# Values times output weights of the second layer, two batches in one product

## The chip, the cores and the metric

The kernel runs on one core of one Trainium2 chip. Its time is the device time of one execution in microseconds (us), taken as the median of 3 runs. The profiled execution is one more execution, of which every row in this document is read. Engines are named as in the profile: PE is TensorE (matmuls), PEld its weight loads, DVE is VectorE, ACT is ScalarE, POOL is GpSimd, SP issues most DMAs.

## What is computed

Four transformer layers on x (4 batches, 256 tokens, 256 features), each a cross-attention on a context of 64 rows per batch and a feed-forward block. The change is in the second layer's attention (L1), of which this is the part that matters:

```python
kv_c = kv @ W_kvc                                  # compressed context, 64 features
k_nope = (kv_c @ W_uk).reshape(b, lk, H, HD)       # H = 16 heads of HD = 128
v = (kv_c @ W_uv).reshape(b, lk, H, HD)
k_rope = rope(kv_c @ W_kr)                         # one for all heads
scores = (q_nope . k_nope + q_rope . k_rope) * scale
attn = softmax(where(good, scores, NEG))
out = einsum('bhqk,bkhd->bqhd', attn, v).reshape(b, lq, H * HD)
return out @ W_o
```

The kernel multiplies each head's values by that head's rows of W_o ahead of the softmax: vo[head, batch] = (kv_c W_uv[head]) W_o[head], 64 context rows by 256 outputs. These tables depend on the context alone and are made long before the second layer begins. They are kept in `a1_vo`, two heads of a pair in one tile of 128 rows: rows 0 to 63 the even head, rows 64 to 127 the odd one.

## The kernel before

The program is written out by hand: every engine has its own instruction order, and semaphores tie them together. A wait holds up all that is behind it on its engine. Helpers such as `products` (line 200) and `turns` (line 209) record most matmuls and transposes, so those have one line for many places.

Three places make the tables of the second layer's attention:

1. Early values, in layer 0's attention (about 34 to 59 us). `layer1_compress_scalar` copies kv_c to `kvc` (line 431). Then heads 0 to 7 pass through a pipeline: PE makes the values of one head (line 487, one product of 256 context columns), ACT copies them to `a_vhead` (line 516), PE multiplies by the output weights (line 498), and ACT copies to `a_vo` (line 506). Line 498 makes one product for each batch: the 64 context rows of the batch are the stationary operand, 256 columns of weights stream. Two batches share a bank, and ACT copies two batches at once: so four products and two copies a head. A product of 32-bit floats leaves two records in the profile, so line 498 has 64 records for 32 products.
2. Keys, in layer 0's feed-forward block (about 65 to 77 us): products of folded weights (line 449) and of `kvc` (line 458), and eight copies on ACT to `a_kq` (line 473).
3. Late values, heads 8 to 15, a step at a time in the loop over the 32 experts of layer 0 (about 125 to 191 us). A head is three steps of the loop: values (line 539), the products of batches 0 and 1, and those of 2 and 3 (line 546). The eight heads take 24 rounds of the loop.

What stands behind the early values: on ACT, in its order, the normalised rows of layer 0's feed-forward (line 304); on PE the transposes of all rows (line 209), then the gate (16 tiles, 32 records, line 200), whose copy on DVE (line 726) begins the routing. DVE and POOL make the other rows (lines 287 and 324). The expert loop gathers rows on POOL (line 1127), and adds the results on POOL (line 1135) by indirect DMAs. In the second layer, DVE sets `a_key_blocks` (line 1341), the block-diagonal rotated keys.

## Time and profile before

| | |
|---|---|
| median of 3 runs | 1147.77 us (1147.11 to 1149.47) |
| profiled execution, span from first to last instruction | 1144.6 us |
| PE busy | 1017.9 us, 89% of the span |
| ACT busy | 632.5 us, 55% |
| DVE busy | 758.7 us, 66% |

The profile gives the profiled execution by its span; its device time is not listed beside it. The median of the runs is 3.2 us above the span, which is taken as what lies around it. A timeline row has start, length, engine, line, operation, and in brackets the idle time of the engine before it and what ended it. The busy share of PE says how full it is over the whole program; what a change of one stage is worth has to be read from the waits of that stage.

### The profile page before, as it was taken

The page shows a single profiled execution, that of the slowest core. Times are in us where ns is not written, and L with a number is a line of the kernel's source. Part 1 is how long each engine was busy: PE and PEld are TensorE (multiplying, and loading weights), DVE is VectorE, ACT ScalarE, POOL GpSimd, SP SyncE. Part 2 cuts the span into 40 slices and gives each one's busy share as a digit, 9 for nine tenths or more (in the row PEclk, how much of TensorE's full clock was granted, in tenths as well). Part 3 has the DMA queues.
Part 4 walks back from the last instruction along what each step waited for, and adds up shares of the span by engine and source line. Part 5 has one row for each costly group of instructions (what it writes and reads, how often), then busy time and mean ns, then how long its engine had stood idle before and what let it go on. Part 6 is the DMA issues. An engine that isn't in the chain of part 4 may idle for free. (4 is left out here: it accounts for less than half of the span.)

```text
span 1144.6 us, 18785 instructions
## 1 busy us (share of the span) xinstructions
PE 1017.9 (89%) x6173; PEld 821.7 (72%) x6173; DVE 758.7 (66%) x2019; ACT 632.5 (55%) x1824; POOL 525.5 (46%) x582
## 2 busy tenths in 40 slices
PE   4987998198998878899999999999999999998997
PEld 2473555156687657788888888989899777677785
DVE  3757222276657347878888888787877689677444
ACT  1341443002124436779787878888888745553253
POOL 1341677254555353334545454444443236452453
PEclk9999999599998898889999999999999999998999
DMA  9130798920004863010102010102000034005674
GB/s 389 50 125 14 190 220 216 251 60 1 1 1 162 273 220 130 1 60 1 61 1 61 1 61 2 60 2 61 1 24 2 1 125 131 1 1 193 216 277 158
DMA packets 57264, 108.89 MB, mean 95 GB/s; under 512 B 13840, under 2 KB 35216, under 8 KB 55248
## 3 DMA queue, kind: packets, MB, share of 16 engines
q1 hardware_dynamic: 47920, 89.71, 23.8%
q0 software_dynamic: 9248, 18.00, 6.1%
q8 instruction: 49, 0.80, 0.3%
q14 instruction: 47, 0.39, 0.1%
HBM read 79.19 MB, written 27.42 MB: 93 GB/s over the span
## 5 line engine op out<-in xcount | busy, mean ns | idle before, releaser
L3028 POOL TENSOR_TENSOR a_p<-a_p,a_tot 128x128 f32<-128x128 f32 x64 | 50.9, 814 | 204.2 <-DVE a_tot L2650 204.2
L200 PE MATMUL bank<-a_w_high,a_in 128*128 128x128 f32 (+1 forms) x512 | 124.4, 285 | 9.6 <-DVE a_in L2167 4.7
L200 PE MATMUL bank<-a_w_low,a_in 128*128 128x128 f32 (+1 forms) x512 | 120.8, 282 | 0.0
L200 PEld LDWEIGHTS bank<-a_w_high,a_in 128*128 128x128 f32 x512 | 99.0, 193 | 12.3 <-DVE a_in L2167 4.5
L200 PEld LDWEIGHTS bank<-a_w_low,a_in 128*128 128x128 f32 x512 | 99.3, 194 | 0.0
L209 PE MATMUL bank<-const 128*128 128x128 f32 x433 | 63.9, 311 | 32.6 <-DVE x L1045 20.5
L209 PEld LDWEIGHTS bank<-const 128*128 128x128 f32 x433 | 59.0, 164 | 36.9 <-DVE x L1045 21.3
L2701 DVE TENSOR_REDUCE a_top<-bank 128x2 f32<-128x512 f32 (+1 forms) x96 | 56.8, 600 | 29.7 <-PE bank L2489 18.0
L2863 ACT ACTIVATE a_qn<-bank,a_q_shift,a_q_rstd 128x128 f32<-128x128 f32 x128 | 48.3, 461 | 40.0 <-POOL a_q_shift L262 40.0
L2679 DVE TENSOR_SCALAR a_qn<-bank,a_qk_minus,a_qk_rstd 128x128 f32<-128x128 f32 x192 | 64.0, 402 | 5.5 <-POOL a_qk_rstd L259 2.8
L200 PE MATMUL bank<-a_proj_high,a_catq 128*128 128x256 f32 x256 | 63.9, 288 | 1.0 <-issue 1.0
L2936 ACT ACTIVATE a_cat<-bank,l_ismooth 128x256 bf16<-128x256 f32 x128 | 50.3, 481 | 23.3 <-PE bank L2529 23.3
L2489 PE MATMUL bank<-a_kt,a_qt 128*128 128x256 f32 x256 | 62.3, 386 | 0.0
L1940 DVE SCALAR_TENSOR_TENSOR f_swi_inner<-bank,f_swi_gated 128x128 f32<-128x128 f32 x78 | 22.4, 290 | 59.5 <-ACT f_swi_gated L1052 59.5
L200 PE MATMUL bank<-a_proj_low,a_catq 128*128 128x256 f32 x256 | 61.7, 279 | 0.0
L200 PE MATMUL bank<-cols,a_vs 128*128 128x256 f32 x256 | 61.1, 382 | 0.0
L2914 ACT ACTIVATE a_p<-bank,a_top 128x256 f32<-128x256 f32 x128 | 59.0, 477 | 0.0
L259 POOL TENSOR_TENSOR rstd<-var,const 128x4 f32<-128x4 f32 x18 | 19.4, 1079 | 85.3 <-DVE minus_mean L253 85.3
L1052 ACT ACTIVATE f_swi_gated<-bank 128x128 f32<-128x128 f32 x78 | 21.5, 277 | 64.8 <-PE bank L200 64.6
L1168 ACT ACTIVATE soft_pt<-bank 128x512 f32<-128x512 f32 x32 | 17.4, 595 | 69.4 <-PE bank L209 69.4
L2855 ACT ACTIVATE a_p<-a_p,a_tot 128x256 f32<-128x256 f32 x128 | 55.5, 540 | 0.0
L209 PE MATMUL bank<-const,a_p 128*128 128x128 f32 x320 | 46.8, 283 | 8.1 <-DVE a_qn L2679 7.4
(427 smaller groups left out, 3039.5 us busy)
## 6 DMA issues: line engine op xcount, KB each, us to landing
experts<-in_experts SPq DMA_DIRECT2D x49, 384.0 KB, 4.4
f_expert<-in_experts SPq DMA_DIRECT2D x31, 384.0 KB, 5.5
third_shelf<-in_groups SPq DMA_DIRECT2D x8, 1024.0 KB, 6.5
f_got<-f_xs SPq DMA_DIRECT2D x10, 516.0 KB, 8.1
third_shelf<-in_groups SPq DMA_DIRECT2D x8, 512.0 KB, 4.3
f_got<-f_ys SPq DMA_DIRECT2D x8, 512.0 KB, 5.3
f_xs<-blank_zero SPq DMA_DIRECT2D x1, 3999.0 KB, 21.3
l_expert<-in_experts SPq DMA_DIRECT2D x10, 384.0 KB, 6.9
```

The lines of the kernel that those rows point to most:

```text
L200: ins = pe.matmul(out, lhs, rhs, start=start and n == 0, stop=stop and n == len(pairs) - 1, skip_group_check=shared)
L209: ins = k.pe.transpose(o, i, ident[0:i.shape[0], 0:i.shape[0]])
L1052: k.a.activation(m.gated[n % 3][0:rows, :], k.bank[n % 3][0:rows, 0:I], ACT.Silu, scale=1.0).then_inc(*s["swi_gated"].one())
L1940: v.scalar_tensor_tensor(m.inner[n % 3][:], bank[n % 3][:, I:2 * I], share, m.gated[n % 3][:], ALU.mult, ALU.mult).then_inc(*s["swi_inner" ...
L2489: ins = pe.matmul(bank[5 + ti][:, h * S:(h + 1) * S], q[:, h, ti * P:(ti + 1) * P], kt[:], start=True, stop=True)
L2679: ins = v.tensor_scalar(dst[i], src[i], m.stats_qk.minus[:, i:i + 1], m.stats_qk.rstd[:, i:i + 1], ALU.add, ALU.mult)
L2701: v.tensor_reduce(top[:, cs], src, AX.X, ALU.max, negate=True).then_inc(*s["top_ready"].one())
L2855: ins = a.activation(p[:, h, :], p[:, h, :], ACT.Copy, scale=tot[:, c:c + 1])
L2863: ins = a.activation(m.qn[:, 0, c, :], bank[3][:, c * P:(c + 1) * P], ACT.Identity, bias=m.stats_q.shift[:, c:c + 1], scale=m.stats_q.rstd ...
L2914: ins = a.activation(own_probs(m, ti)[:, h, :], bank[5 + ti][:, h * S:(h + 1) * S], ACT.Exp, bias=top[:, c:c + 1], accum_out=tot[:, c:c + 1])
L2936: ins = a.activation(m.cat[n % 2][:, c * S:(c + 1) * S], bank[h][:, part * S:(part + 1) * S], ACT.Copy, scale=m.ismooth[:, ch:ch + 1])
L3028: g_.tensor_tensor(cross_probs(m, ti), cross_probs(m, ti), over(m.tot[n % 2][:, first:first + HPG], SC), ALU.mult).then_inc(*s["cross_weig ...
```

## The change

For each head one product now takes the 128 context rows of two batches as the stationary operand. Its output has the first batch of the two in rows 0 to 63 of a bank and the second in rows 64 to 127. To keep the two heads of a pair in the two halves of one tile, the odd heads are made from a copy of kv_c in which the two batches of each couple are exchanged (`kvc_crossed`, two more copies on ACT). So in batches 0 and 2 the even head lies in the upper half of a pair's tile, in batches 1 and 3 the odd head does. The keys follow: within a pair the two heads are exchanged in batches 1 and 3, for `a_kq` by the place to which the key products write and two half-size copies for one, for `a_key_blocks` by four instructions in place of two. Copies to `a_vo` stay two for each head, each of 64 rows by 512. A late head is now two steps of the expert loop, and ACT makes both its copies in one step.

```diff
--- before.py
+++ after.py
@@ -428,6 +428,9 @@
 def layer1_compress_scalar(k, s):
     k.on_a.wait_ge(*s["kvc_made"].at(1))
+    sides = lambda ap: ap.rearrange("p (c d s) -> p c d s", c=B // 2, d=2)
+    for d in range(2):
+        k.a.activation(sides(k.kvc_crossed[:])[:, :, d, :], sides(k.bank[5][0:KVC, 0:CTX])[:, :, 1 - d, :], ACT.Copy)
     k.a.activation(k.kvc[:], k.bank[5][0:KVC, 0:CTX], ACT.Copy).then_inc(*k.kvc_copied.one())
@@ -453,10 +456,12 @@
         bank = k.bank[KEY_BANKS[n % len(KEY_BANKS)]]
         on.wait_ge(*s["fold_copied"].at(max(2 * n // FOLD, n % len(KEY_BANKS)) + 1))
         on.wait_ge(*k.kq_scaled.at(n - len(KEY_BANKS) + 1))
+        kvc = k.kvc[:].rearrange("p (c d s) -> p d c s", c=B // 2, d=2)
+        parts = bank[0:QC, :].rearrange("p (q c s) -> p q c s", q=4, c=B // 2)
         for i in range(2):
             h = 2 * n + i
-            ins = pe.matmul(bank[0:QC, i * CTX:(i + 1) * CTX], fold[:, h * QC:(h + 1) * QC], k.kvc[:], start=True,
-                            stop=True)
+            ins = pe.matmul(parts[:, 1:3, :, :] if i else parts[:, 0:4:3, :, :], fold[:, h * QC:(h + 1) * QC], kvc,
+                            start=True, stop=True, skip_group_check=True)
         ins.then_inc(*s["keys_made"].one())
@@ -470,8 +475,10 @@
 def layer1_keys_scalar(k, s):
     for n in range(H1 // 2):
         k.on_a.wait_ge(*s["keys_made"].at(n + 1))
-        k.a.activation(k.kq[:, :, 2 * n:2 * n + 2, :], k.bank[KEY_BANKS[n % len(KEY_BANKS)]][0:QC, :].rearrange(
-            "p (h b s) -> p b h s", h=2, b=B), ACT.Copy, scale=SOFT1).then_inc(*k.kq_scaled.one())
+        bank = k.bank[KEY_BANKS[n % len(KEY_BANKS)]][0:QC, :].rearrange("p (d h c s) -> p d c h s", d=2, h=2, c=B // 2)
+        for d in range(2):
+            ins = k.a.activation(k.kq[:, d::2, 2 * n:2 * n + 2, :], bank[:, d, :, :, :], ACT.Copy, scale=SOFT1)
+        ins.then_inc(*k.kq_scaled.one())
 def layer1_values_tensor(k, s, pair_free):
@@ -484,27 +491,33 @@
     for r in range(EARLY + 1):
         if r < EARLY:
             on.wait_ge(*s["vhead_copied"].at(r - 1))
-            pe.matmul(k.bank[6 + r % 2][:, 0:CTX], uv[:, r, :], k.kvc[:], start=True,
+            pe.matmul(k.bank[6 + r % 2][:, 0:CTX], uv[:, r, :], kept_context(k, r), start=True,
                       stop=True).then_inc(*s["vhead_made"].one())
         if r >= 1:
             i = r - 1
-            lo = (i % 2) * SC
             on.wait_ge(*s["vhead_copied"].at(i + 1))
-            for pair in range(B // 2):
-                n = 2 * i + pair
-                on.wait_ge(*(pair_free[n] if n < 4 else k.vo_copied.at(n - 3)))
-                for b in range(2):
-                    at = (pair * 2 + b) * SC
-                    ins = pe.matmul(k.bank[1 + n % 4][lo:lo + SC, b * D:(b + 1) * D], k.vhead[i % 3][:, at:at + SC],
-                                    wo[:, i, :], start=True, stop=True)
-                ins.then_inc(*s["wo_made"].one())
-def value_out_scalar(k, h, pair, bank):
-    lo = (h % 2) * SC
-    k.a.activation(k.vo[lo:lo + SC, pair * 2:pair * 2 + 2, h // 2, :],
-                   bank[lo:lo + SC, :].rearrange("p (b d) -> p b d", b=2), ACT.Copy).then_inc(*k.vo_copied.one())
+            on.wait_ge(*(pair_free[i] if i < 4 else k.vo_copied.at(2 * (i - 3))))
+            value_out_tensor(k, s, i, wo[:, i, :], k.bank[1 + i % 4])
+def kept_context(k, h):
+    return k.kvc_crossed[:] if h % 2 else k.kvc[:]
+def value_out_tensor(k, s, i, wo, bank):
+    for c in range(B // 2):
+        ins = k.pe.matmul(bank[:, c * D:(c + 1) * D], k.vhead[i % 3][:, c * P:(c + 1) * P], wo, start=True, stop=True)
+    ins.then_inc(*s["wo_made"].one())
+def value_out_scalar(k, h, bank):
+    for side in range(2):
+        part, d = slice(side * SC, (side + 1) * SC), (side + h) % 2
+        k.a.activation(k.vo[part, d::2, h // 2, :], bank[part, :].rearrange("p (c d) -> p c d", c=B // 2),
+                       ACT.Copy).then_inc(*k.vo_copied.one())
 def layer1_values_scalar(k, s):
@@ -512,51 +525,44 @@
     for r in range(EARLY + 1):
         if r < EARLY:
             on.wait_ge(*s["vhead_made"].at(r + 1))
-            on.wait_ge(*s["wo_made"].at(2 * (r - 2)))
+            on.wait_ge(*s["wo_made"].at(r - 2))
             a.activation(k.vhead[r % 3][:], k.bank[6 + r % 2][:, 0:CTX],
                          ACT.Copy).then_inc(*s["vhead_copied"].one())
         if r >= 1:
-            for pair in range(B // 2):
-                n = 2 * (r - 1) + pair
-                on.wait_ge(*s["wo_made"].at(n + 1))
-                value_out_scalar(k, r - 1, pair, k.bank[1 + n % 4])
-LATE = 3 * (H1 - EARLY)
+            on.wait_ge(*s["wo_made"].at(r))
+            value_out_scalar(k, r - 1, k.bank[1 + (r - 1) % 4])
+LATE = 2 * (H1 - EARLY)
 def late_value_tensor(k, s, step, bank):
     pe, on = k.pe, k.on_pe
-    i, part = divmod(step, 3)
-    lo = ((EARLY + i) % 2) * SC
+    i, part = divmod(step, 2)
     if part == 0:
         on.wait_ge(*k.l1_in)
         on.wait_ge(*k.vo_copied.at(2 * (EARLY + i)))
         uv = k.l1["uv_late"][0:KVC, :].rearrange("p (h d) -> p h d", d=HD1)
-        pe.matmul(bank[:, 0:CTX], uv[:, i, :], k.kvc[:], start=True, stop=True).then_inc(*s["vhead_made"].one())
+        pe.matmul(bank[:, 0:CTX], uv[:, i, :], kept_context(k, EARLY + i), start=True,
+                  stop=True).then_inc(*s["vhead_made"].one())
     else:
         wo = k.l1["wo_late"].rearrange("p (h d) -> p h d", d=D)
         on.wait_ge(*s["vhead_copied"].at(i + 1))
-        on.wait_ge(*k.vo_copied.at(2 * (EARLY + i) + part - 1))
-        for b in range(2):
-            at = ((part - 1) * 2 + b) * SC
-            ins = pe.matmul(bank[lo:lo + SC, b * D:(b + 1) * D], k.vhead[i % 3][:, at:at + SC], wo[:, i, :],
-                            start=True, stop=True)
-        ins.then_inc(*s["wo_made"].one())
+        value_out_tensor(k, s, i, wo[:, i, :], bank)
 def late_value_scalar(k, s, step, bank):
-    i, part = divmod(step, 3)
+    i, part = divmod(step, 2)
     if part == 0:
         k.on_a.wait_ge(*s["vhead_made"].at(i + 1))
-        k.on_a.wait_ge(*s["wo_made"].at(2 * (i - 2)))
+        k.on_a.wait_ge(*s["wo_made"].at(i - 2))
         k.a.activation(k.vhead[i % 3][:], bank[:, 0:CTX], ACT.Copy).then_inc(*s["vhead_copied"].one())
     else:
-        k.on_a.wait_ge(*s["wo_made"].at(2 * i + part))
-        value_out_scalar(k, EARLY + i, part - 1, bank)
+        k.on_a.wait_ge(*s["wo_made"].at(i + 1))
+        value_out_scalar(k, EARLY + i, bank)
 VALUES = dict(pe="vhead_made wo_made", a="vhead_copied")
@@ -1338,8 +1344,10 @@
     on.wait_ge(*step.now())
     on.wait_ge(*s["keys_zeroed"].at(1))
     for h in range(2):
-        ins = v.tensor_scalar(m.key_blocks[h * R1:(h + 1) * R1, :, h * SC:(h + 1) * SC],
-                              by_b(m.turn_a[h * R1:(h + 1) * R1, :]), SOFT1, None, ALU.mult)
+        for d in range(2):
+            at = (h + d) % 2
+            ins = v.tensor_scalar(m.key_blocks[h * R1:(h + 1) * R1, d::2, at * SC:(at + 1) * SC],
+                                  by_b(m.turn_a[h * R1:(h + 1) * R1, :])[:, d::2, :], SOFT1, None, ALU.mult)
     ins.then_inc(*s["keys_set"].one())
     def rotate(half):
@@ -3586,6 +3594,7 @@
         k.expert_in, k.experts_first = [k.landing(f"expert{n}_in") for n in range(SLOTS)], 0
         k.route1 = sparse_routing(k, SPARSE1, ctx)
         k.kvc = k.sb("a1_kvc", [KVC, CTX], scope=l1_scope)
+        k.kvc_crossed = k.sb("a1_kvc_crossed", [KVC, CTX], scope=l1_scope)
         k.kq = k.sb("a1_kq", [QC, B, H1, SC], scope=l1_scope)
         k.vo = k.sb("a1_vo", [P, B, H1 // 2, D], scope=l1_scope)
         l1 = k.sb("l1_weights", [P, width(L1A)], scope=l1_scope)
```

How the order changes on PE in the early values, from the compression (line 200) on. Before, line 487 makes values and line 498 multiplies by output weights:

```order
L200 MATMUL bank<-ctxt,l_key_weights 64x256 x2
L487 MATMUL bank<-a_kvc,l_value_weights 128x256 x2
L498 MATMUL bank<-l_value_weights,a_vhead 64x256 x4
L487 MATMUL bank<-a_kvc,l_value_weights 128x256
L498 MATMUL bank<-l_value_weights,a_vhead 64x256 x4
L487 MATMUL bank<-a_kvc,l_value_weights 128x256
L498 MATMUL bank<-l_value_weights,a_vhead 64x256 x4
```

The same place of the changed kernel (lines 494 and 511 do this now):

```order
L200 MATMUL bank<-ctxt,l_key_weights 64x256 x2
L494 MATMUL bank<-a_kvc,l_value_weights 128x256
L494 MATMUL bank<-a_kvc_crossed,l_value_weights 128x256
L511 MATMUL bank<-l_value_weights,a_vhead 128x256 x2
L494 MATMUL bank<-a_kvc,l_value_weights 128x256
L511 MATMUL bank<-l_value_weights,a_vhead 128x256 x2
L494 MATMUL bank<-a_kvc_crossed,l_value_weights 128x256
```

The order of the heads is the same; each group of four products with 64 output rows is a group of two with 128 output rows.

How the order changes on ACT, from the last instruction ahead of the compressed context on. Before:

```order
L660 ACTIVATE l_seq<-bank,l_weights 128x256 x2
L431 ACTIVATE a_kvc<-bank 64x256
L516 ACTIVATE a_vhead<-bank 128x256 x2
L506 ACTIVATE a_vo<-bank 64x2x256 x2
L516 ACTIVATE a_vhead<-bank 128x256
```

The same place of the changed kernel:

```order
L433 ACTIVATE a_kvc_crossed<-bank 64x2x64 x2
L434 ACTIVATE a_kvc<-bank 64x256
L529 ACTIVATE a_vhead<-bank 128x256 x2
L519 ACTIVATE a_vo<-bank 64x2x256 x2
L529 ACTIVATE a_vhead<-bank 128x256
```

Two copies stand ahead of that of kv_c, and the rest keeps its order.

How the order changes on PE in the expert loop, at the first late head (line 539 makes its values, line 546 multiplies). Before:

```order
L539 MATMUL bank<-a_kvc,l_weights 128x256
L209 MATMUL bank<-const,f_pick 128x96 x2
L200 MATMUL bank<-experts,f_cols 96x256 x2
L209 MATMUL bank<-const,swi_inner 128x96
L931 MATMUL bank<-experts,swi_turned 96x256
L546 MATMUL bank<-l_weights,a_vhead_2 64x256 x2
L209 MATMUL bank<-const,f_pick 128x96 x2
L200 MATMUL bank<-experts,f_cols 96x256 x2
L209 MATMUL bank<-const,swi_inner 128x96
L931 MATMUL bank<-experts,swi_turned 96x256
L546 MATMUL bank<-l_weights,a_vhead_2 64x256 x2
```

The same place of the changed kernel:

```order
L549 MATMUL bank<-a_kvc,l_weights 128x256
L209 MATMUL bank<-const,f_pick 128x96 x2
L200 MATMUL bank<-experts,f_cols 96x256 x2
L209 MATMUL bank<-const,swi_inner 128x96
L937 MATMUL bank<-experts,swi_turned 96x256
L511 MATMUL bank<-l_weights,a_vhead_2 128x256 x2
L209 MATMUL bank<-const,f_pick 128x96 x2
L200 MATMUL bank<-experts,f_cols 96x256 x2
L209 MATMUL bank<-const,swi_inner 128x96
L937 MATMUL bank<-experts,swi_turned 96x256
L549 MATMUL bank<-a_kvc_crossed,l_weights 128x256
```

One round of every three no longer has late work of its own: 16 rounds have it, not 24.

## Rows read from the trace of the kernel before

**Rows 1.** Timeline, PE, ahead of the early values (start, length, engine, line, what)

```profile
19.38 2.07 PE L200 MATMUL bank<-l_weights,l_mean_wide 128*128 128x256 f32 x4 [3.68 <-DVE l_mean_wide L627]
21.38 1.22 PE L200 MATMUL bank<-l_weights,const 1*128 1x256 f32 x2
22.53 2.08 PE L200 MATMUL bank<-l_weights,l_mean_wide 128*128 128x256 f32 x4
```

**Rows 2.** Timeline of PE and ACT in the early values, heads 0 to 2

```profile
33.99 0.38 ACT L431 ACTIVATE a_kvc<-bank 64x256 f32<-64x256 f32 x1 [17.42 <-PE bank L200]
...
36.49 3.67 PE L498 MATMUL bank<-l_value_weights,a_vhead 128*64 128x256 f32 x8
...
38.49 0.59 ACT L506 ACTIVATE a_vo<-bank 64x512 f32<-64x512 f32 x1 [1.51 <-PE bank L498]
...
41.24 3.67 PE L498 MATMUL bank<-l_value_weights,a_vhead 128*64 128x256 f32 x8
...
45.54 1.94 PE L498 MATMUL bank<-l_value_weights,a_vhead 128*64 128x256 f32 x8
```

**Rows 3.** Timeline, a later head, the end of the early values, and ACT's rows

```profile
48.04 1.94 PE L498 MATMUL bank<-l_value_weights,a_vhead 128*64 128x256 f32 x8
...
49.15 0.59 ACT L506 ACTIVATE a_vo<-bank 64x512 f32<-64x512 f32 x1 [0.62 <-PE bank L498]
...
50.53 1.49 PEld L498 LDWEIGHTS bank<-l_value_weights,a_vhead 128*64 128x64 f32 x8 [0.33 <-issue]
...
54.60 1.32 POOL L324 TENSOR_SCALAR rows<-x,minus_mean,rstd 128x256 f32<-128x256 f32 x2
...
57.51 1.69 ACT L506 ACTIVATE a_vo<-bank 64x512 f32<-64x512 f32 x3 [0.27 <-PE bank L498]
59.22 1.09 ACT L304 ACTIVATE rows<-x,shift,rstd 128x256 f32<-128x256 f32 x2
```

**Rows 4.** Timeline, transposes, gate, and the key copies

```profile
60.03 1.94 PE L209 MATMUL bank<-const,rows 128*128 128x128 f32 x16 [1.64 <-issue]
...
61.88 3.73 PE L200 MATMUL bank<-l_weights,cols 128*128 128x32 f32 x32
...
65.71 0.42 DVE L726 COPY f_logits<-bank 128x256 f32<-128x256 f32 x1 [3.45 <-PE bank L200]
...
75.39 0.59 ACT L473 ACTIVATE a_kq<-bank 96x512 f32<-96x512 f32 x1 [0.27 <-PE bank L458]
```

**Rows 5.** Stretches of PE: start:end, length, busy (records), granted clock, DMA share, GB/s

```profile
19.38:22.53 3.15, 3.15 (x7) 1.00 1.03 402
...
41.24:44.90 3.66, 3.66 (x10) 1.00 0.00 0
...
61.85:65.50 3.65, 3.65 (x34) 1.00 1.06 346
65.50:68.90 3.40, 3.40 (x22) 0.50 0.98 359
227.85:232.70 4.85, 4.82 (x23) 0.50 1.10 322
```

**Rows 6.** Timeline, fill transposes at either pace, and PE's wait for the mask

```profile
77.01 7.21 PE L209 MATMUL bank<-const 128*128 128x128 f32 x64
...
87.61 0.28 PE L869 MATMUL bank<-f_mask,f_before 128*128 128x256 bf16 x1 [3.39 <-DVE f_mask L982]
...
227.88 5.62 PE L209 MATMUL bank<-const 128*128 128x128 f32 x28 [20.53 <-DVE x L1045]
```

**Rows 7.** Expert loop: timeline of POOL and a small ACT copy; a line of the waits

```profile
124.07 0.27 ACT L1052 ACTIVATE swi_gated<-bank 96x128 f32<-96x128 f32 x1 [2.15 <-PE bank L200]
...
175.95 1.44 POOL L1135 DMA_INDIRECT sum<-f_ys,f_index  x1 [0.30 <-ACT f_ys L1100]
...
178.93 1.44 POOL L1135 DMA_INDIRECT sum<-f_ys,f_index  x1 [0.30 <-DMA sum<-f_ys,f_index]
...
ACT f_ys L1100 <- DMA sum<-f_ys,f_index: 23.7, 12, 3.6
```

## Prediction

> **What bounds the kernel here.** I read the timeline of the three places that the change touches, then PE's pace in stretches, then the waits of the expert loop. In the early values PE is the bound: ACT's copies to `a_vo` wait for PE (1.51 us, later 0.62 us), and ACT ends them at 57.51 + 1.69 = 59.20 [rows 2, 3]. Only then can ACT make its rows (59.22), which the transposes at 60.03 wait for, though POOL had its last rows ready at 54.60 + 1.32 = 55.92 [rows 3, 4]. Transposes, gate and routing follow in one chain to DVE's copy at 65.71. So a us at the end of the early values is a us of the kernel, down to a floor: with ACT early, POOL's rows (the first of the two ends near 55.3) let the transposes begin at about 55.5, 4.5 us sooner.
>
> The reader must see a second thing, PE's pace. A group of eight records of 256 columns takes 3.67 us at 36.49 and 41.24, and 1.94 us from 45.54 on [rows 2]. That is the lower and the higher level of PE's clock, 1.2 and 2.4 GHz; the granted clock is printed as 1.00 even in the slow stretches (19.38 and 41.24), so here the durations tell the level [rows 5]. What had PE done? From 19.38 on it worked in groups of four records and two, with a pause at each border: 22.53 - 19.38 = 3.15 us for six records, which at 0.427 each ((3.67 - 1.94)/8 = 0.216 is what a record loses, so 0.43 is the low pace) are 2.56 us of work [rows 1, 2]. It printed as busy throughout and stayed slow for 25 us. It rose right after the second unbroken group of eight. Later, at 65.5, the clock fell behind the gate, whose products have only 32 columns, and was up again at 77, after denser work [rows 4 to 6].
>
> **The change, part by part.**
>
> Two copies of `kvc` with exchanged batches stand ahead of the one that starts the values. The trace has none of 64 x 128; an ACT copy of 96 x 128 takes 0.27 [rows 7], 64 x 256 takes 0.38 [rows 2]. Two cost 0.4 to 0.76; I take 0.5. PE's first output product moves from 36.49 to 37.0.
>
> The output products. Four records of 128 stationary columns stand where eight of 64 did; a record is paid by its 256 streamed columns, as the wide stationary of rows 1 and the narrow one of rows 2 both run at 0.43 at the low pace. At the high pace a head took 50.53 - 48.04 = 2.49 us [rows 3] and would take 2.49 - 4 x 0.216 = 1.63. At the low pace a head took 41.24 - 36.49 = 4.75 [rows 2] and would take what the six records of rows 1 take, 3.15.
>
> The question is which pace PE gets, and this decides the sign. With the change no group of eight is left before the last head: each round is four records, a pause, two records, a pause, and the two are of 64 rows only. This is the pattern of rows 1, which never brought the clock up, not that of 41.24, after which it rose. So I take the low pace for all the early values.
> - Output products of head 0 at 37.0, of head 6 at 37.0 + 6 x 3.15 = 55.9, of head 7 right behind at 55.9 + 4 x 0.43 = 57.6. A first copy starts 2.0 behind its group's start (38.49 - 36.49) [rows 2]: 59.6. Two copies take 1.1 (three took 1.69) [rows 3]. End 60.7 instead of 59.2: +1.5.
> - Transposes: 61.88 - 60.03 = 1.85 for 16 before [rows 4]. A low transpose is 5.62/28 = 0.20, a high one 7.21/64 = 0.11 [rows 6]: 16 x 0.20 = 3.2. +1.4.
> - Gate: 3.73 for 32 records, 0.117 each [rows 4]. That is the pace of a 128-column transpose, so the load of 128 stationary columns rather than the 32 streamed ones seems to set it, and it would become 0.20: 6.4. +2.7. No row shows a gate at the low clock. If something else sets the 0.117, the term is 0.
> - Sum 1.5 + 1.4 + 2.7 = +5.6, with the clock low to the end of the gate. But the last two heads' output products are now together an unbroken eight records (55.9 to 59.3), and the 16 transposes are an unbroken 3.2. Either can bring the clock up as the eight at 41.24 did; then part of the 4.1 of transposes and gate goes. I take off 1.6: +4.0.
>
> The Trainium skill has a rule against the change: in "TensorE: Matmul & The Clock Gate", section "A second HAM failure mode: psum-queue depth-cycling", short idles of PE between groups of matmuls are said to cost it the higher clock. By that rule the early values run slow; the rows above agree as far as groups of four and two go. The same page, section "Step-by-step: what each phase is for", gives 62 ns of sequencer time for a MATMUL; an estimate by it makes the gate bound by issue, with no growth at the low clock, and the sum +2.9 or less.
>
> The keys. ACT's eight copies of 96 x 512 (0.59, each behind a wait of 0.27 for PE) become sixteen of 96 x 256, a pair about 2 x 0.38 = 0.76, inside the 0.86 that PE takes for a pair [rows 4]. Only the last pair ends later, by 0.2; PE then waits 3.39 for the mask, which covers it [rows 6]. The writes of the key products in pieces of 64 columns: 0, or, if it slowed them by a tenth, 0.7, under the same cover. If PE were still slow in the keys, 7 us would be added to 3.4 of slack; but the folded weights ahead of them are dense, and brought the clock up before [rows 5].
>
> `a_key_blocks`: two instructions more on DVE, 0.1 each; PE rotates queries meanwhile and DVE catches up. 0, or +0.2.
>
> The late values. Eight heads lose two products each, 16 x 0.43 = 6.9 us of PE. POOL sets the loop's pace: its additions come 178.93 - 175.95 = 2.98 apart, and ACT's copies of results wait 23.7 us in 12 times for those DMAs [rows 7]. So PE's saving is hidden: 0. ACT makes both copies in one step, 0.5 more in that round and less in others, under the same cover. If PE were the bound, -6.9; if ACT's longer step delayed additions, +1.
>
> **The sum** against the profiled execution is 1144.6 + 4.0 = 1148.6 of span. With the 3.2 us around it that stand between its span and the median, 1147.77 + 4.0 = 1151.8.
>
> **The rivals.**
>
> *The clock rises as before* (PE keeps working nearly all the time, and it rose at 45). Then heads 0, 1 and 2 start at 37.0, 40.2 and 43.3, head 3 at 46.1, and from there 1.63 a head: head 6 at 51.0, head 7 at 51.9, first copy 1.11 later (49.15 - 48.04) [rows 3], end 54.1. Now POOL's rows bind, transposes at 55.5 instead of 60.0: -4.5, 1143.3. Against it: the pattern of rows 1. For it: PE is printed as busy through all of it, and one rise is little to judge by. Chance 0.22.
>
> *The gain comes in the expert loop*, PE's 6.9 us counting in full on top of +4.0: 1144.9. Against it POOL's 2.98 [rows 7]. Chance 0.03.
>
> *The clock rises in the last eight records and stays up* through transposes and gate: only the 1.5 is left, 1149.3, within the noise. The pause behind them (ACT's two copies and its row, about 2 us) speaks against it. Chance 0.12.
>
> **How the numbers follow.** The forecast, low clock through the early values and in part or all of what follows, has 0.63; its own range is 1150.2 to 1154.0 (+2.4, the clock up from the transposes' end, to +6.2, with the dearer copies and all terms). The range for 8 in 10 reaches from 1144.0, into the early-rise case, to 1154.0. About 0.2% (2.3 us) can be told from no change here. Faster 0.25, same 0.13, slower 0.62.
>
> **What would show it.** In the profile after: groups of four output records (line 511) with about 2.0 us each, heads 3.1 apart to the end; ACT's last copy of the early values near 60.7; transposes of 0.2 and a gate of over 5 us; DVE's copy of the logits near 69 to 71 instead of 65.7. The additions on POOL should still be 2.98 apart, with PE's idle share in the loop larger. The prediction is wrong if line 511 runs in groups of 1.1 us from about 45 on and the transposes start near 55.5; and its mechanism is wrong if the logits come no later than before and the loss lies in the expert loop or behind.

## The result, and the profile after

| kernel | runs | median us | range us |
|---|---|---|---|
| before | 6 | 1148.24 | 1147.11 to 1149.47 |
| after | 6 | 1155.65 | 1151.13 to 1158.98 |

The ratio is 1.0065, 95% interval [1.0047, 1.0083]: slower by 7.4 us, where 4.0 were forecast and 1154.0 was the end of the range. The profiled execution of the changed kernel was its fastest (1151.13 us, span 1149.6); the kernel before had a span of 1144.6. A second profile of each was taken later with unchanged code (spans 1153.9 and 1148.1), and the table below has all four. It gives the us from one event to the next, in order of time (starts, but for the first row); the columns add up to the spans to within 0.1.

| from the event before to | before | before, again | after | after, again |
|---|---|---|---|---|
| end of ACT's last early copy to `a_vo` | 59.2 | 59.1 | 60.5 | 60.8 |
| DVE's copy of the logits | 6.5 | 6.5 | 7.1 | 11.3 |
| first product with the mask | 21.9 | 21.9 | 21.9 | 21.9 |
| POOL's first gather | 22.9 | 22.9 | 23.9 | 24.0 |
| POOL's first addition | 17.7 | 17.7 | 21.1 | 21.0 |
| POOL's last addition | 81.9 | 82.8 | 81.7 | 81.4 |
| end | 934.5 | 937.2 | 933.5 | 933.6 |

All of the loss is ahead of the first addition: 6.2 us in the first pair (134.42 instead of 128.2), 10.9 in the second. Behind it 1.2 and 5.1 us came back, so that the spans are 5.0 and 5.8 us apart; no run explains that part. The early values answer as forecast. The timeline of the changed kernel (start, length, engine, line, what):

```profile
33.72 0.43 ACT L433 ACTIVATE a_kvc_crossed<-bank 64x128 f32<-64x128 f32 x2 [17.43 <-PE bank L200]
...
36.53 2.07 PE L511 MATMUL bank<-l_value_weights,a_vhead 128*128 128x256 f32 x4
38.64 1.21 ACT L519 ACTIVATE a_vo<-bank 64x512 f32<-64x512 f32 x2 [1.62 <-PE bank L511]
...
39.69 2.08 PE L511 MATMUL bank<-l_value_weights,a_vhead 128*128 128x256 f32 x4
...
52.30 2.07 PE L511 MATMUL bank<-l_value_weights,a_vhead 128*128 128x256 f32 x4
...
55.45 3.78 PE L511 MATMUL bank<-l_value_weights,a_vhead 128*128 128x256 f32 x8
...
59.27 1.21 ACT L519 ACTIVATE a_vo<-bank 64x512 f32<-64x512 f32 x2 [0.50 <-PE bank L511]
60.50 1.09 ACT L304 ACTIVATE rows<-x,shift,rstd 128x256 f32<-128x256 f32 x2
```

Beside [rows 2, 3]: no group ever takes 1.1 us; heads start 3.15 apart from 36.53 to 52.30, on half the records and all at the lower level, where the kernel before had 1.94 for eight records from 45.54 on. The two crossed copies took 0.43 us. Transposes, gate and logits, here and (second fence) in the second execution:

```profile
61.31 1.94 PE L209 MATMUL bank<-const,rows 128*128 128x128 f32 x16 [2.08 <-issue]
...
63.15 4.31 PE L200 MATMUL bank<-l_weights,cols 128*128 128x32 f32 x32
...
67.57 0.42 DVE L732 COPY f_logits<-bank 128x256 f32<-128x256 f32 x1 [4.03 <-PE bank L200]
...
73.94 0.65 ACT L480 ACTIVATE a_kq<-bank 96x256 f32<-96x256 f32 x2 [0.55 <-PE bank L463]
```

```profile
61.60 3.65 PE L209 MATMUL bank<-const,rows 128*128 128x128 f32 x16 [2.08 <-issue]
65.04 6.87 PE L200 MATMUL bank<-l_weights,cols 128*128 128x32 f32 x32
...
72.02 0.42 DVE L732 COPY f_logits<-bank 128x256 f32<-128x256 f32 x1 [6.90 <-PE bank L200]
```

Beside [rows 4]: the clock rose at 59.3 in the first execution, just behind the last eight output records, and not before 77 in the second. In the second, the gate takes 6.87 us for 3.73: the dearer of the two prices that the prediction gave it. Stretches of the changed kernel (start:end, length, busy, then the granted clock, the DMA share, GB/s):

```profile
36.52:52.30 15.78, 15.78 (x32) 8.37 (x31) 14.94 (x44) 7.67 (x15) 7.12 (x10) 0.50 0.14 48
59.28:66.10 6.82, 4.79 (x43) 4.71 (x43) 1.38 (x2) 3.46 (x6) 5.12 (x12) 1.00 0.45 149
66.10:72.90 6.80, 6.80 (x40) 6.51 (x40) 0.87 (x3) 4.82 (x8) 6.80 (x3) 0.50 1.00 351
113.90:117.30 3.40, 3.40 (x10) 2.61 (x10) 0.59 (x3) 0.77 (x3) 2.52 (x3) 0.50 0.26 68
127.60:131.00 3.40, 3.40 (x10) 2.35 (x11) 0.66 (x3) 0.27 (x1) 0.00 (x0) 0.50 0.91 361
```

The last two are what the prediction did not look at. They lie between the first gather and the first addition, where PE has the shared expert's products and then those of the first gathered rows. The clock fell there for 3.4 us twice. The first product of gathered rows in the kernel before:

```profile
122.96 1.07 PE L200 MATMUL bank<-experts,f_cols 128*96 128x256 f32 x4 [0.38 <-DVE f_cols L1031]
```

and after:

```profile
127.53 1.97 PE L200 MATMUL bank<-experts,f_cols 128*96 128x256 f32 x4 [0.38 <-DVE f_cols L1037]
```

In the expert loop, POOL's additions keep their pace. From the first to the last of them PE is busy for 62.2 us of 81.7, where it was 71.2 of 81.9: PE's saving of the late values became waiting.

```profile
176.24 1.44 POOL L1141 DMA_INDIRECT sum<-f_ys,f_index  x1 [0.31 <-DVE swi_inner L1044]
...
179.22 1.44 POOL L1141 DMA_INDIRECT sum<-f_ys,f_index  x1 [0.30 <-issue]
```

ACT's waits for those additions, over the whole program (us, times, longest), were 30.2 in 15 times before; the 23.7 of [rows 7] are those up to 200 us only:

```profile
ACT f_ys L1106 <- DMA sum<-f_ys,f_index: 38.5, 16, 4.3
```

### The profile page after: what moved, and what is told of

Its sections match the earlier page's. It is cut to its first block and busy times, and to the rows that moved or that the text cites. A ratio compares the mean times of both kernels' runs of the same rounds, so it can differ in the third digit from the quotient of the medians.

```text
span 1149.6 us, 18669 instructions
## 1 busy us (share of the span) xinstructions
PE 1013.0 (88%) x6109; PEld 824.8 (72%) x6109; DVE 758.5 (66%) x2021; ACT 632.8 (55%) x1834; POOL 525.5 (46%) x582
## 3 DMA queue, kind: packets, MB, share of 16 engines
q1 hardware_dynamic: 47920, 89.71, 23.9%
## 5 line engine op out<-in xcount | busy, mean ns | idle before, releaser
L209 PE MATMUL bank<-const 128*128 128x128 f32 x433 | 60.8, 300 | 33.8 <-DVE x L1051 21.5
L209 PEld LDWEIGHTS bank<-const 128*128 128x128 f32 x433 | 55.3, 157 | 37.8 <-DVE x L1051 21.9
L200 PE MATMUL bank<-cols,a_vs 128*128 128x256 f32 x256 | 60.5, 380 | 0.0
L259 POOL TENSOR_TENSOR rstd<-var,const 128x4 f32<-128x4 f32 x18 | 19.4, 1079 | 85.1 <-DVE minus_mean L253 85.1
L2863 ACT ACTIVATE a_p<-a_p,a_tot 128x256 f32<-128x256 f32 x128 | 55.5, 539 | 0.0
```

Source lines behind the costliest of these rows:

```text
L200: ins = pe.matmul(out, lhs, rhs, start=start and n == 0, stop=stop and n == len(pairs) - 1, skip_group_check=shared)
L209: ins = k.pe.transpose(o, i, ident[0:i.shape[0], 0:i.shape[0]])
L2863: ins = a.activation(p[:, h, :], p[:, h, :], ACT.Copy, scale=tot[:, c:c + 1])
```

## The experiments

Ratios are to the kernel before, run in the same session (its medians there were 1146.2 to 1147.4; one execution of it, of 3477 us, is in no ratio), with 95% intervals. "The change" is the changed kernel. "..." marks lines of an edit that are left out here. Where two kernels of one pair are compared, the difference of their means is worked out from their runs, with twice its error.

**One. Undo the products' form.** In the changed kernel each product of 128 rows becomes two of 64, in the early values (first), the late ones (second), or both (third).

```
...
-        ins = k.pe.matmul(bank[:, c * D:(c + 1) * D], k.vhead[i % 3][:, c * P:(c + 1) * P], wo, start=True, stop=True)
+        for d in range(2 if split else 1):
+            n = SC if split else P
+            at = c * P + d * n
+            ins = k.pe.matmul(bank[d * n:(d + 1) * n, c * D:(c + 1) * D], k.vhead[i % 3][:, at:at + n], wo,
+                              start=True, stop=True)
...
```

> The changed kernel, with each early output product (heads 0 to 7) made again as two products of 64 rows, each to its half of the same bank; all else as changed. Pace theory: groups of eight records are back, PE rises to its higher level within the early values as before, ACT's last copy ends near 59 to 60, the logits are copied near 66, and the time is 1147 to 1150. Rival, the late values (both copies in one step of the expert loop) cost the time: 1154 to 1157, as the changed kernel. Rival, the side changes (exchanged copies of kv_c, key copies halved) cost it: also 1154 to 1157.

> The changed kernel, with each late output product (heads 8 to 15, in the expert loop) made as two products of 64 rows; early ones as changed. Pace theory: 1154 to 1157, as the changed kernel, with groups of four at 2.08 us to the end of the early values. Rival, a PE that is too idle in the expert loop loses its pace there and costs the time: 1148 to 1151.

> The changed kernel with all output products split in two of 64 rows: PE's work as before, all side changes and the late order as changed. Pace theory: 1147 to 1150, as the early split alone. Rival, side changes or the order of ACT's late copies: 1154 to 1157.

Measured: 1151.06 us, 1.0037 [1.0022, 1.0051]; 1153.37, 1.0048 [1.0029, 1.0067]; 1149.89, 1.0030 [1.0013, 1.0046]. The second is just below its range of 1154 to 1157. The third lies in the range of the pace theory (1147 to 1150) and the first just above it, but not for the theory's reason, for neither is an undoing at all. The early values' timeline of the first:

```profile
36.74 1.97 PE L514 MATMUL bank<-l_value_weights,a_vhead 128*64 128x256 f32 x8
38.64 1.22 PE L494 MATMUL bank<-a_kvc,l_value_weights 64*128 64x256 f32 x2
39.79 1.97 PE L514 MATMUL bank<-l_value_weights,a_vhead 128*64 128x256 f32 x8
```

Eight records take 1.97 us at the lower level, where eight of the kernel before took 3.67 [rows 2]: the two products of a pair write to different halves of the bank's rows and run at the same time, while before, both batches of a head went to the same half. So PE is as short of work as with the change, and its clock stayed low through the early values: to 73.5 in the first, to 59.2 in the third, whose transposes and most of whose gate then ran at the higher level. Why both are 3 to 4 us nearer to the kernel before than the change (1.0065, and 1.0073 in its second session) is not shown: ACT's last early copy ends only 0.5 us sooner (60.0 and 59.9). For the late values the form makes no difference that the intervals can tell.

**Two. Give PE back its work.** Each early output product of the changed kernel is made twice in a row.

```
...
-    for c in range(B // 2):
+    for c in [c for c in range(B // 2) for _ in range(times)]:
...
```

> Each early output product is made twice in a row into the same place, so that TensorE has again eight records of 256 columns without a break per head, as before, while everything else is the change's (the second product repeats the first; nothing else differs). Theory (a dense group of eight brings the clock up): groups of 3.67 us for the first heads, the clock up by about 45, groups of 1.94 from there, ACT's last copy to a_vo at 59 to 60, logits at 65 to 67, time 0.998 to 1.002 of before: more work and yet faster than the change. Rival 1 (TensorE's clock is not decided by the pattern of work here): it stays low, eight heads of 4.75 us end at 76, and the time is 15 us above before. Rival 2 (the loss of the change is the two copies to kvc_crossed or ACT's form of the output copies): the clock rises and the time is still 1.005 of before.

Measured: 1150.13 us, 1.0036 [1.0017, 1.0055]; by its means 4.3 +- 2.0 us faster than the change in the same session, though it makes the early output products twice, and 3.3 +- 2.1 slower than the kernel before. Its PE:

```profile
36.40 3.77 PE L511 MATMUL bank<-l_value_weights,a_vhead 128*128 128x256 f32 x8
40.10 0.70 PE L494 MATMUL bank<-a_kvc,l_value_weights 64*128 64x256 f32 x2
40.73 1.99 PE L511 MATMUL bank<-l_value_weights,a_vhead 128*128 128x256 f32 x8
...
59.28 2.48 PE L209 MATMUL bank<-const,rows 128*128 128x128 f32 x16 [2.08 <-issue]
61.56 6.87 PE L200 MATMUL bank<-l_weights,cols 128*128 128x32 f32 x32
```

The clock rose at 40.0, at the end of the first group. The forecast of the time (0.998 to 1.002) missed: the clock fell again at 60.5, in the transposes, and the gate took 6.87, so the logits came at 68.5. PE's idle time ahead of the transposes is 2.08 here and with the change, 1.64 before [rows 4]; whether that made it fall is argued, since in one execution of the change, and in the third kernel of experiment one, it stayed up behind the same wait.

**Three. The order alone, in the kernel before.** The next head's value product is cut into two of 128 columns, one ahead of each pair of batches, so that eight output records become four and four.

```
...
+            at = slice(part * P, (part + 1) * P)
+            ins = pe.matmul(k.bank[6 + r % 2][:, at], uv[:, r, :], k.kvc[:, at], start=True, stop=True)
...
             for pair in range(B // 2):
+                if pair == 1:
+                    head(r, 1)
...
```

> The kernel before, without any fill, and only its order changed: the next head's value product is made in two halves of 128 columns, one ahead of each pair of batches, so that the eight output records of a head are two groups of four with a short product of 64 rows between them. The sum of the work is the same but for the switches. Theory (TensorE's clock rises on an unbroken group of eight records and not on groups of four): it stays low through the early values, a head takes 5.1 us, eight end at about 77, 15 to 18 us later than before: 1.012 to 1.016 of before. Rival (what counts is how much of the time is spent in products of 128 rows, broken or not; the change lowered that share by halving them): the clock rises between 40 and 50 as before, and the time is 1.001 to 1.004 of before.

Measured: 1150.36 us, 1.0037 [1.0021, 1.0054]. Its PE:

```profile
38.58 1.97 PE L507 MATMUL bank<-l_value_weights,a_vhead 128*64 128x256 f32 x4
40.48 0.79 PE L488 MATMUL bank<-a_kvc,l_value_weights 64*128 64x128 f32 x2
41.20 1.74 PE L507 MATMUL bank<-l_value_weights,a_vhead 128*64 128x256 f32 x4
42.87 0.48 PE L488 MATMUL bank<-a_kvc,l_value_weights 64*128 64x128 f32 x2
43.28 1.08 PE L507 MATMUL bank<-l_value_weights,a_vhead 128*64 128x256 f32 x4
```

The clock rose at 42.6 without any unbroken eight of output records. My theory of the unbroken group falls, and the rival's number (1.001 to 1.004) holds. What PE did ahead of each rise within the early values is the same in the four executions that have one (the kernel before twice, this one, and that of experiment two): the output products of a head take the time of eight records one after the other (3.94 us of a head's 5.25 here). In the five without a rise (the change twice, the three of experiment one) they take the time of four (2.07 of 3.15 with the change, 1.97 of 3.05 in the first of experiment one). These nine executions show it; that it is the cause rests on them alone. The rule that the prediction cited from the Trainium skill, "TensorE: Matmul & The Clock Gate", section "A second HAM failure mode: psum-queue depth-cycling", blames short idles between groups. This kernel has twice as many borders between groups of output products as the one before and its clock rose earlier (42.6, not 45.0), so by this case the number of pauses doesn't decide.

**Four. Bring the clock up by other means, with and without the change.** 18 transposes into a free bank go behind the product of the sequence summaries, where PE waits for DVE.

```
     ins.then_inc(*s["seq_made"].one())
+    pass_time(k, k.bank[7], 18)
```

> The changed kernel, with 18 fill transposes on PE between the first products and the summaries, where PE waits 3.7 us for DVE (about 15.7 to 19.4 us). Pace theory: PE gets to its higher level near 18 and holds it through groups of four and two; summaries take 7 us instead of 12.6, heads 1.6 us instead of 3.15, DVE and POOL then set the start of the transposes at about 49 to 51 us, and the time is 1139 to 1145. Rival, the level does not hold in groups of four and two: it falls back by 25 us, and the time is 1153 to 1157. Rival, the loss is in the expert loop: the logits come 10 us earlier but the time only by that less 3 to 5 us of loss in the loop.

> The kernel before with 18 idle-time transposes behind the product of the sequence summaries, the same that brought the changed kernel's clock up from 17.3 us on and its time to 0.9965 of before. With the clock up in both, this pair tells what the change is worth in itself. Early values at the high pace from head 0: 2.49 us a head before against 1.69 with the change, so ACT's last copy to a_vo at about 33.7 + 8 x 2.5 + 2 = 49 instead of 42.9; POOL's rows (ready near 50 then) hide that. Theory (the saving of the output products is hidden behind POOL's rows once the clock is up): 0.9955 to 0.998 of before, no more than 1.5 us from the changed kernel with the same fill. Rival (the change has a cost of its own, in the keys or the late values): 2 us or more faster than that kernel, 0.9945 or less.

Measured, with the change: 1143.73, 0.9965 [0.9945, 0.9985]. Without it: 1140.12, 0.9943 [0.9923, 0.9963]. The clock is up from about 17 us on in both, so the early values end at 42.9 and 47.4, and both wait for POOL's rows at 49.7. The groups of four and two that never raised the clock keep it up here, from 29.2 to the end of the early values. Only in the filled kernels can the saving of the output products be seen: 4.5 us, all of it waiting. With the change, PE idles 8.16 us, its clock falls at 44.6, and the transposes and the gate are at the lower level throughout (logits at 60.2). Without it PE idles 3.06 us, the clock falls at 50.8, in the transposes, and the gate is as slow (logits at 59.0). The means are 3.4 +- 2.2 us apart, which is the number of the rival (the change has a cost of its own) and not the theory's 1.5. In the profiles 1.1 us of it are there at the logits, and 3.6 more came between gather and addition (21.3 and 17.7 us), where the clock of the kernel with the change was low in two stretches and that of the other in none. The transposes with the change:

```profile
48.70 1.32 POOL L324 TENSOR_SCALAR rows<-x,minus_mean,rstd 128x256 f32<-128x256 f32 x2
49.73 3.65 PE L209 MATMUL bank<-const,rows 128*128 128x128 f32 x16 [8.16 <-POOL rows L324]
```

**Five. Cover that idle time too** (60 transposes with the change, 24 without), and then (third and fourth) also the waits ahead of the mask, of the shared experts' weights and of their first inner product.

```
+    pass_time(k, k.bank[7], 60)
     turn_rows_tensor(k, s, k.rows, rows_of(s), k.x_ready[NT - 1])
...
-    pass_time(k, k.bank[4], 64)
+    pass_time(k, k.bank[4], 82)
...
+    pass_time(k, k.bank[0], 16)
     slot, came = expert_slot(k, 0)
...
+            pass_time(k, k.bank[7], 14 if r == 1 else 0)
             on.wait_ge(*s["swi_inner"].at(i + 1))
```

> The change, with 18 idle-time transposes behind the sequence summaries (as in the two earlier pairs) and 60 more in TensorE's idle time of 8 us ahead of the row transposes, where the clock fell. Theory (transposes and gate take 1.85 + 3.73 at the higher clock): row transposes at 49.7, logits at about 55.4 instead of 60.2, so 4.8 us less than with the first fill alone: 0.9915 to 0.994 of before. Where the shared experts fall into a stretch of low clock, 3 us of it go again. Rival (the fill delays the row transposes or the clock falls all the same): logits at 60 or later, 0.9965 or more.

> The kernel before with the same two fills, the second of 24 transposes, since TensorE is idle only 3.06 us there. Theory: logits at about 55.4 instead of 59.0, 3.6 us less than with the first fill alone, 0.990 to 0.993 of before, and within 1.5 us of the changed kernel with two fills (TensorE's shorter early values end in waiting for POOL's rows). Rival (the change has a cost of its own beside the clock): 2 us or more faster than the changed kernel with two fills.

> The change with those two fills and three more places covered: 82 transposes instead of 64 ahead of the mask, 16 between the last picks and the shared experts' weights, 14 in the wait for the first inner product. Theory (the 3 us that the shared experts took longer in some executions are TensorE's clock, which falls in these waits): mask to first gather 22.9, first gather to first addition 17.7 instead of 21, 0.988 to 0.991 of before, the fastest of the changed ones. Rival (that stretch is longer by the change itself, for instance by DMAs): 21 us again with the clock up throughout.

> The kernel before with all five fills. Theory (with the clock held up everywhere ahead of the expert loop the change is worth nothing either way, since POOL's rows and POOL's additions bound both): within 1.5 us of the changed kernel with all fills, first addition at the same time within 1 us. Rival 1 (the change costs by itself): 2 us or more faster than that. Rival 2 (the change helps once the clock is up): 2 us or more slower.

Measured, two fills: 1141.00, 0.9973 [0.9948, 0.9998] with the change, 1137.52, 0.9932 [0.9905, 0.9960] without. All five: 1139.11, 0.9947 [0.9923, 0.9970] with, 1137.20, 0.9924 [0.9894, 0.9953] without. Both kernels with the change missed the forecast of their ratio (0.9915 to 0.994, and 0.988 to 0.991). Yet the profiles are alike: logits at 55.2 to 55.6 in all four, and with five fills the first addition at 119.9 in both and a span of 1138.3 in both. This is the first addition with the change and five fills:

```profile
119.89 1.50 POOL L1145 DMA_INDIRECT sum<-f_ys,f_index  x1 [4.21 <-ACT f_ys L1110]
```

With the clock up, the stretch from gather to addition is 17.7 with the change as well; the rival of a longer stretch by DMAs falls. But the medians are 3.5 us apart with two fills and 1.9 with five (means 4.6 +- 2.5 and 2.4 +- 2.5), beyond the 1.5 of the theory: three of twelve executions of each kernel with the change lie at 1144 to 1149.5, with a mean granted clock of 0.94 to 0.955, where the others have 0.951 to 0.963. None of these was profiled. Such times are not the change's alone: with one fill the kernel before had one of 1147.43.

**Six. Denser work ahead of the early values.** The first fill gets 26 transposes, and 6 (4 without the change) fill the wait for kvc. Against the kernels with five fills:

```
+    pass_time(k, k.bank[7], 6)
...
-    pass_time(k, k.bank[7], 18)
+    pass_time(k, k.bank[7], 26)
```

> The change with all five fills, the first made longer (26 transposes instead of 18, so that TensorE does not idle ahead of the summaries) and a sixth of 6 transposes in the wait for kvc. With five fills its 12 runs had a median of 1139.1 but three of them lay at 1144 to 1147 with 0.01 less granted clock, which the kernel before did not show. Theory (in those executions the clock fell back ahead of the early values, and the change's groups of four and two did not bring it up again): with denser work ahead of them the slow executions go, the runs lie between 1135 and 1141, and the median within 1 us of the kernel before with the same fills. Rival (they come from a place behind the early values): again one run in four above 1143.

> The kernel before with the same six fills (4 transposes in the wait for kvc, which is shorter there): the partner of the run above. Theory: 1136 to 1139, no different from its partner by more than 1 us. Rival (the change costs by itself even with the clock up): 2 us or more faster than its partner.

Measured: 1138.86 (1137.71 to 1141.63), 0.9931 [0.9912, 0.9950] with the change; 1137.54 (1136.37 to 1138.32), 0.9915 [0.9897, 0.9932] without. None of six runs was above 1141.7, nearly as the theory had it (1141), though six are few to exclude one in four. The means are 1.6 +- 1.3 us apart, where the theory allowed 1 and the rival asked for 2: neither is settled. The spans of the profiled executions are 1136.6 and 1136.4. The last has the lowest ratio of this study, and it doesn't hold the change.

**Seven. Late products twice**, on top of the sixth pair's changed kernel.

> The changed kernel with the six fills, and each output product of the late values made twice, so that TensorE has as much of them in the expert loop as before the change (the second repeats the first). Theory (the late saving is hidden behind POOL's additions, and the loss is none of it): the same time as its partner without the repetition, within 1 us, additions 2.98 us apart. Rival 1 (less work in the loop lets TensorE's clock fall there and costs time): this kernel is 1.5 us or more faster. Rival 2 (the saving counts after all): it is 2 us or more slower.

Measured: 1138.47, 0.9922 [0.9903, 0.9940]; by its means 0.8 +- 1.5 us faster than without the repetition. Neither a gain nor a cost of the late values' saving shows, down to about 2 us.

**Both kernels again**, as controls.

> The changed kernel once more, in the same session as the other three. Theory (the early values keep TensorE at its lower clock, and with it the transposes and the gate or the shared experts behind them): 1.0035 to 1.008 of before, line 511's groups 3.15 us apart up to 52, and DVE's copy of the logits somewhere from 67.5 to 71.5. What lies behind the logits (the wait for the first gather, the shared experts) should scatter by 3 us or so between executions of the same code. Rival (the loss is a fixed cost of the late values or behind them): the same milestones as in the first execution, and a first addition 23.9 + 21 us behind the mask again.

> The kernel before once more as a control: 0.9985 to 1.0015 of before. Its second trace tells what repeats: theory expects the clock's rise within the early values again, between 40 and 50, line 498's groups at 1.94 from there, and the logits at 65 to 67. If its clock stays low up to the transposes in this trace, the rise at 45 was chance and the theory of the change's loss needs another cause.

Measured: 1154.10, 1.0073 [1.0051, 1.0095], and 1147.03, 1.0000 [0.9982, 1.0017]. By the durations the clock of the kernel before rose at 44.9 in the second trace and at 45.0 in the first. With the change the logits came at 72.0, past the expected 71.5, and what lies behind the mask repeated (24 + 21 us), against the expected scatter.

## Why the prediction was right in sign and too small

**The pace of the early values: right, for a wrong reason.** ACT's last copy ended at 60.5, 60.7 was forecast: +1.3 for +1.5 (+1.7 in the second pair). The clock stayed low, as the pattern of [rows 1] said. The reason given, no unbroken group of eight, fell with experiment three: what the change took away is half of the output records per head. The prediction also overlooked that PE's work begins with an unbroken eight:

```profile
11.86 3.47 PE L200 MATMUL bank<-ctxt,l_weights 128*128 128x256 f32 x8 [11.86 <-DMA ctxt<-in_ctx]
```

In 13 of the 18 profiled executions these take 3.75 us, here 3.47, so the clock rose at their end; its fall is on record at 18.3, in PE's wait of 3.77 us ahead of the summaries. The clock had been up before the groups of four and two began.

**Transposes and gate: a middle value, where each execution is at one side.** The forecast took 1.6 off +1.4 and +2.7 and had +2.5. The two executions of the change gave +0.6 and +4.7. The full terms were right where the clock stays low: 3.65 and 6.87 us in the second execution. In the five profiled executions whose clock was low through all the early values (the change twice, the three of experiment one) logits came 7.1, 11.3, 11.3, 8.2 and 6.7 us behind ACT's last copy, where 6.5 were needed before. So 2.5 is near the mean of what they add, though none of the five had it. The gate's 6.87 us at the lower level, seen in five kernels, settle what no row of before showed. The estimate by the Trainium skill's 62 ns for a MATMUL ("TensorE: Matmul & The Clock Gate", section "Step-by-step: what each phase is for"), which had the gate unchanged, does not hold here: a record takes 0.117 us at the higher level and 0.215 at the lower. It could have been seen before: 32 records at 62 ns are 2.0 us, and [rows 4] has 3.73.

**The step that failed: the stages behind the logits were put at nothing.** The prediction's sum stopped at the logits and gave no reason. In both executions of the change the stretch from mask to first gather took 1.0 and 1.1 us longer, and that from gather to first addition 3.4 and 3.3: about 4.4 us that the sum lacks. The second part is the clock. Over all 18 profiled executions that stretch took 17.7 us in the nine whose clock stayed up in it, 19.2 to 19.4 in the six with 3.4 us of low clock, and 21.0 to 21.3 in the three with 6.8 to 7.6 us. Of the first part, 0.3 us are the clock, low in the fill transposes behind the mask (3.83 us instead of 2.16). The other 0.7 to 0.8 are DVE's wait for a DMA:

```profile
112.36 0.19 DVE L1018 TENSOR_TENSOR f_number<-f_table 96x32 f32<-96x32 f32 x1 [3.60 <-DMA f_table<-f_pick]
```

It is 3.60 and 3.70 us in the two executions of the change, 2.91 and 2.90 in those of the kernel before, and 2.9 to 3.0 in five others with the change's layout; its cause is open. Of the code there nothing is changed. Low clock between gather and addition came in 8 of 11 profiled executions with the change's layout and in 1 of 7 without; why so much more often is not shown.

So the first pair of profiles has 1.3 + 0.6 + 1.0 + 3.4 us at the first addition and the second 1.7 + 4.7 + 1.1 + 3.3, of which 1.2 and 5.1 come back behind it. How the 7.4 us between the medians divide is not known, since the other executions have no profile.

**The rest: right.** The keys' copies took 0.65 a pair and are hidden (PE still waits 2.39 for the mask, 3.39 before [rows 6]). The late saving is hidden: additions 2.98 apart. The rival of a clock that rises as before did not occur; its other half, POOL's rows as the floor, is what experiments four and five show, at 49.7 instead of the 55.5 assumed, since POOL came earlier too once the clock was up. The 3.2 us taken to lie around the span were too much: in the changed kernel's profiled execution it is 1.5 (1151.13 and 1149.6), and in none of its six more than 1.6. By that, the profiled execution of the kernel before lay some 1.7 us below the median of its runs; the forecast of a difference does not hang on it.

**Does the change cost by itself, the clock aside?** In all four pairs with fills the kernel with the change is slower by its means. With the clock up nearly everywhere 1.6 +- 1.3 us remain, and the profiled spans are 0.2 us apart. In that pair the clock still fell once between gather and addition with the change (first addition 121.1, without it 119.2). So what is left is at most about 3 us, and may be nothing but such falls.

## What to carry to other kernels

On a path where TensorE's clock is not up from the start, halving its work can be a loss: here it paid the saving back at half pace, there and in the next stages. Before a product is made wider, see from the durations at which level the stage runs, and whether the engine ends the wait at all at the higher level; here POOL's rows and POOL's additions did. And follow the clock past the stage that is changed: the terms that the sum lacked lie in code that the change doesn't touch. Filling TensorE's waits with transposes into a free bank gave 0.85% of the whole time, more than any form of the products.

## What the runs showed of the hardware

- Two products of 64 stationary columns whose results go to different halves of the bank's rows ran at the same time: eight records in 1.97 us, against 3.67 when both go to the same half. This is what the Trainium skill's "TensorEngine Tiling (Array Packing)", section "Key Properties", says of tiles: different ones can work in parallel, and each is tied to its partitions; the trace agrees. The kernel before might have had the change's saving by order alone, with two heads' products side by side. That was not tried.
- A gate of 32 columns with a stationary operand of 128 columns takes nearly twice as long at the lower level (3.73 and 6.87 us), so it is not paid by an issue time that the clock leaves alone. Nor by its streamed columns: 0.117 us a record is what a transpose with 128 of them takes (0.113).
- 18 transposes in PE's wait of 3.7 us kept PE at work where the clock otherwise was seen to fall (at 18.2 to 19.6 us in six executions). They took 2.1 to 3.0 us, less than the 3.6 of the lower level, so by about 17 us the clock was up, and it stayed up to the end of the early values.
- The granted clock is no measure of the early part: the second kernel of experiment one ran all its early values at the lower level (2.07 us for four records) with 1.00 printed beside them. The change has 41 us at half speed on record there (18.3 to 59.3), which is 0.018 of its mean of 0.940; the other's mean is 0.955.
